# Attention and mixture-of-experts kernel: prologue and turn 0 written out by hand, and up's first high half moved from ScalarE to GpSimd

## The reference

```python
x = x + xattn(layernorm(x), ctx)          # q = xn Wq' + bq, k = ctx Wk' + bk, v = ctx Wv' + bv, softmax(q k' / sqrt(128)) v
h = layernorm(x)
probs = softmax(h router_w')
a_h = gelu(h actor_w1' + actor_b1)
k = argmax(clip(a_h actor_w2' + actor_b2, -30, 30)) + 1
scores = where(rank(probs) < k, probs, 0)
for e in range(8):
    out += scores[e] * ((silu(h gate_w[e]') * (h up_w[e]')) down_w[e]')
x = x + out
```

## Time and profile before

| what | value |
|---|---|
| median of 3 runs | 747.63 us (747.62 to 747.85) |
| the profiled execution | 748.23 us |
| its span | 746.3 us |
| PE busy | 736.3 us, 99% |
| DVE, ACT, POOL busy | 637.8, 558.8, 588.5 us |
| granted PE clock | 1.00 (2.4 GHz) in every stretch |

### The profile page before, as it was taken

The page is one execution under the profiler, slowest core; times in us unless marked ns, Lnnn a source line. Parts: engine busy times, 40 slices in busy tenths (PEclk is TensorE's granted clock), DMA queues, the critical chain, the costliest instruction groups (busy, mean ns, idle before and its releaser), DMA issues.

```text
span 746.3 us, 13836 instructions
## 1 busy us (share of the span) xinstructions
PE 736.3 (99%) x3680; PEld 363.5 (49%) x3680; DVE 637.8 (85%) x1407; ACT 558.8 (75%) x990; POOL 588.5 (79%) x616
## 2 busy tenths in 40 slices
PE   8999999999999999999999999999999999999998
PEld 4544454544545445454544545445454544444445
DVE  7899888897888889888898988889888897978777
ACT  5998787777877767777777777767777777877664
POOL 2686979789796887979698796887979688687763
PEclk9999999999999999999999999999999999999999
DMA  9200311314043142332424243152322323120110
GB/s 346 68 27 1 78 36 43 59 28 92 9 112 67 50 109 56 98 55 79 88 41 98 54 112 66 46 110 55 98 55 78 78 42 85 35 51 14 30 29 29
DMA packets 128511, 50.49 MB, mean 68 GB/s; under 512 B 106832, under 2 KB 117072, under 8 KB 128464
## 3 DMA queue, kind: packets, MB, share of 16 engines
q1 hardware_dynamic: 128032, 49.47, 27.8%
q10 hardware_dynamic: 432, 0.48, 0.2%
HBM read 28.92 MB, written 13.40 MB: 57 GB/s over the span
## 4 chain that ended last, share of the span: by engine, by line
PE 92%; ACT 2%; DVE 2%; issue 1%; DMA 1%; SPq 0%; POOL 0%; DVEq 0%; ACTq 0%; POOLq 0%
PE bank L690 28%; PE bank L692 28%; PE bank L691 28%; PE bank L586 2%; PE bank L557 2%; DMA raw_gate<-in_gate_t 1%; PE bank L651 1%; PE bank L670 1%; PE bank L594 1%; PE bank L593 1%; PE bank L595 1%; DVE bank L1663 0%; ACT up_hi L885 0%; DVE hid_lo L1669 0%; ACT down_hi L885 0%
## 5 line engine op out<-in xcount | busy, mean ns | idle before, releaser
L1288 POOL TENSOR_TENSOR weighted<-silu,score_bc 128x512 f32<-128x512 f32 x336 | 430.7, 1298 | 86.2 <-ACT silu L1037 81.7
L1663 DVE SCALAR_TENSOR_TENSOR bank<-bank,h_scale,weighted 128x512 f32<-128x512 f32 x336 | 253.5, 754 | 82.1 <-PE bank L692 66.8
L1031 ACT ACTIVATE hid_hi<-bank 128x512 f16<-128x512 f32 x336 | 200.8, 598 | 147.0 <-DVE bank L1663 144.9
L1037 ACT ACTIVATE silu<-bank,silu_scale 128x512 f32<-128x512 f32 x336 | 230.7, 687 | 23.3 <-PE bank L692 23.1
L1669 DVE TENSOR_TENSOR hid_lo<-bank,hid_hi 128x512 f16<-128x512 f32 x336 | 227.7, 678 | 0.0
L690 PE MATMUL bank<-xn_lo,gate_hi 128*128 128x512 f16 x336 | 127.6, 380 | 1.1 <-ACT silu L1037 1.0
L690 PE MATMUL bank<-xn_lo,up_hi 128*128 128x512 f16 x336 | 127.4, 379 | 1.2 <-DVE hid_lo L1669 0.9
L692 PE MATMUL bank<-xn_hi,up_hi 128*128 128x512 f16 x336 | 127.3, 379 | 0.0
L691 PE MATMUL bank<-xn_hi,up_lo 128*128 128x512 f16 x336 | 127.3, 379 | 0.0
L692 PE MATMUL bank<-xn_hi,gate_hi 128*128 128x512 f16 x336 | 127.3, 379 | 0.0
L691 PE MATMUL bank<-xn_hi,gate_lo 128*128 128x512 f16 x336 | 127.3, 379 | 0.0
(11 more groups left out here) (220 smaller groups left out, 809.6 us busy)
## 6 DMA issues: line engine op xcount, KB each, us to landing
x_in<-in_x SPq DMA_DIRECT2D x16, 256.0 KB, 2.8
y_kept<-y_sb SPq DMA_DIRECT2D x60, 64.0 KB, 2.6
y_tok<-y_kept SPq DMA_DIRECT2D x15, 256.0 KB, 2.8
out<-out_sb SPq DMA_DIRECT2D x15, 256.0 KB, 2.2
xt_in<-in_x_t SPq DMA_DIRECT2D x14, 256.0 KB, 2.9
row_bc<-row_kept SPq DMA_DIRECT2D x14, 256.0 KB, 4.0
ctx_in<-in_ctx_t SPq DMA_DIRECT2D x14, 240.0 KB, 2.9
v_kept<-raw_gate SPq DMA_DIRECT2D x10, 256.0 KB, 2.0
```

Source lines behind the costliest of these rows:

```text
L1031: af(hid_hi[j % HRING][:], up_bank[j % U_BANKS][:], ACT.Copy).then_inc(hid_hi_ready, 1)
L1037: af(silu[j % RING][:], gate_bank[(par + j) % G_BANKS][:], ACT.Silu, scale=silu_scale[:])\
L1288: g.tensor_tensor(weighted[j % RING][:], silu[j % RING][:], score_bc[par][:], ALU.mult)\
L1663: v.scalar_tensor_tensor(up_bank[j % U_BANKS][:], up_bank[j % U_BANKS][:], h_scale[:], weighted[j % RING][:], ALU.mult, ALU.mult).then_inc ...
```

## The change

Prologue and turn 0 are now one list of calls on each of PE, ACT, POOL and DVE; the loop over `j` begins with turn 1. On SP nothing changes. The tables of turn 0 and the helpers that made its exceptions are gone. No instruction is left out. One changes its engine: the high half of part 1 (up's first 7 tiles) is made by POOL. `value_bias(2)` goes from turn 0 into POOL's prologue, and block 1's values wait on `v_ready` (2) where they had a semaphore of their own.

```diff
 @block.tensor
+            values(0, 0, up_bank[2])
+            energies(0)
             keys(1, 1, up_bank[1])
-            energies(0)
-            values(0, 0, up_bank[2])
+            probs_transposes(0)
             values(1, 1, y_bank)
-            probs_transposes(0)
             attend(0)
...
-            gate(0, 0, 1)
-            gate(0, 0, 2)
-            score_transposes(0)
+            attend(1, y_bank)
             pe.wait_ge(kmin_ready, 1)
             keys(5, 1, x1)
+            gate(0, 0, 1)
+            score_transposes(0)
             score_broadcast(0)
-            attend(1, y_bank)
             up(0, 0, 0)
+            gate(0, 0, 2)
             up(0, 0, 1)
             gate(0, 0, 3)
+            gate(0, 0, 4)
             up(0, 0, 2)
...
 @block.scalar
             tanh(0)
-            keys(4, up_bank[0])
             exps(1)
-            weight_high(1)
+            weight_sums(7)
             router_exps(0)
+            keys(3, gate_bank[1])
+            turned_probs(1, up_bank[1])
             nc.scalar.preload_act_table(ACT.Silu)
             gated(0, 0, 0)
-            turned_probs(1, up_bank[1])
+            keys(4, up_bank[0])
             weight_high(2)
...
 @block.gpsimd
             rstd_2(0)
-            weight_high(0, 0, FIRST_TILES)
+            value_bias(2)
+            weight_high(0, 0, 2)
             x2_low(0, 0)
-            weight_high(0, FIRST_TILES, PART)
+            weight_high(0, 2, 7)
             route_probs(0)
+            weight_high(1, 0, 7)
             rank_over(0)
             pool.wait_ge(s16_ready, 1)
             rstd_1(2, 0)
             weigh(0, 0, 0)
+            weigh(0, 0, 1)
+            rstd_2(1)
+            weigh(0, 0, 2)
+            weigh(0, 0, 3)
+            weigh(0, 0, 4)
+            weigh(0, 0, 5)
+            add_row(2)
+            weigh(0, 0, 6)
...
+            weigh(0, 0, 12)
+            x2_low(1, 1)
+            route_probs(1)
...
 @block.vector
             weight_magnitude(0)
+            row_max(0)
             weight_magnitude(1)
-            row_max(0)
             row_below(0)
...
             router_sum(0)
+            values(1, y_bank)
             actor_count(0)
-            stats_1(2, 0, 2, BB)
             route_ahead(0)
             route_rank(0)
+            row_sum(1)
+            scores(0)
+            split_scores(0)
             aggregate_1_waits(2)
             aggregate_1(2)
-            scores(0)
-            split_scores(0)
-            values(1, y_bank)
             weight_low(1)
-            row_sum(1)
-            residual(1, 1, 0, BB, y_bank)
+            residual(1, 1, 0, 4, y_bank)
...
+            down_actor_scales()
+            weight_low(2)
+            hidden(0, 3)
+            low(0, 2)
+            weight_low(3)
+            hidden(0, 4)
+            low(0, 3)
+            hidden(0, 5)
+            low(0, 4)
+            weight_low(4)
...
```

More of the change, by code:

```diff
@@ L366, in turns @@
         def turns(eng, turn):
-            for t in range(LOOP_FIRST):
+            for t in range(1, LOOP_FIRST):
                 turn(t, t % 2)
@@ L1293, in turn @@
                 for j in range(TILES):
[L1295 removed]
+                    if j == 11 and is_block(t + 1):
                         route_probs(t + 1)
@@ new lines, in _ @@
+            stats_2_waits(1)
+            stats_2(1)
+            aggregate_2_waits(1)
+            aggregate_2(1)
+            hidden(0, 0)
+            weight_tops(1, 2, 3)
+            hidden(0, 1)
+            low(0, 0)
+            low(0, 1)
+            weight_top(1, 2, 4)
+            hidden(0, 2)
+            down_actor_scales()
[6 more added lines that the diff above has]
+            hidden(0, 5)
@@ new lines, in _ @@
+            low(0, 4)
+            weight_low(4)
+            low(0, 5)
+            hidden(0, 6)
+            actor_arg(1)
+            hidden(0, 7)
+            low(0, 6)
+            row_max(2)
+            actor_gelu(1)
+            weight_low(5)
+            row_base(2, 0)
+            hidden(0, 8)
+            hidden(0, 9)
+            low(0, 7)
+            router_less(1)
+            weight_low(6)
+            low(0, 8)
+            hidden(0, 10)
+            low(0, 9)
+            actor_logits(1)
@@ new lines, in _ @@
+            stats_1(3, 1)
+            actor_count(1)
+            hidden(0, 11)
+            low(0, 10)
+            router_sum(1)
+            weight_low(7)
+            hidden(0, 12)
+            low(0, 11)
+            low(0, 12)
+            aggregate_1_waits(3)
+            aggregate_1(3)
+            hidden(0, 13)
+            route_ahead(1)
+            hidden(0, 14)
+            row_sum(2)
+            weight_low(8)
+            route_rank(1)
+            hidden(0, 15)
+            low(0, 13)
@@ new lines, in _ @@
+            low(0, 14)
+            low(0, 15)
+            residual(2, 0, 0, 2)
+            scores(1)
+            hidden(0, 16)
+            residual(2, 0, 2, 4)
+            hidden(0, 17)
+            low(0, 16)
+            stats_2_waits(2)
+            stats_2(2)
+            hidden(0, 18)
+            low(0, 17)
+            aggregate_2_waits(2)
+            aggregate_2(2)
+            hidden(0, 19)
+            low(0, 18)
+            low(0, 19)
+            hidden(0, 20)
+            actor_low()
```

322 lines of the change are left out of this document (206 added, 116 removed).

## The result

| | kernel before | changed kernel |
|---|---|---|
| median | 747.63 us (747.40 to 747.96, 5 runs) | 752.31 us (751.66 to 753.16, 5 runs) |
| ratio | | 1.0063, 95% interval 1.0051 to 1.0074 |
| profiled execution | 748.23 us, span 746.3 | 752.31 us, span 750.5 |
| first up product | 33.00 us | 35.65 us |
| turn 1's first product, T0 | 79.71 us | 83.63 us |

The change makes the kernel 0.6% slower: 4.7 us where I forecast 0.3, and 2.7 us above the top of the range. Nearly all of it lies ahead of T0, as the prediction said: in the two profiled executions T0 moved by 3.92 us and the span by 4.2. The profiled executions lie 4.1 us apart and the medians 4.7, because that of the kernel before took 0.6 us more than its median and that of the changed kernel took just its median.

The account below looks back on a forecast made before the run. PE, busy for 99% of the span, was taken as the bound. First up product +1.0 us, one gate product more +0.65, fewer turn 0 stalls -1.4: +0.25 on 747.63 gives 747.9 us, range 746.3 to 749.6.

Parts of the forecast that it names:

- Only T0 can move: Whole kernel: PE has no gap from turn 1's first product (79.71 us), so only that start can move.
- `ahead` is held by POOL's high half: Prologue, DVE: ready at 28.6 us, `ahead` waits for POOL's `up_hi` until 30.4, some 2 us instead of 0.42.
- rival 2: Turn 0: low halves hit `add_row(2)` (part 3) and `weighted` 11 (part 6); 749.0 or 749.9 us; chance 0.20.
- "`value_bias(2)`" had no price: Turn 0: counted only as taken out of POOL's middle; no cost given for its new place in the prologue.
- `values(1)` fits into the wait for `probs_t`: nothing: Prologue, PE: `values(1)`, moved behind the transposes at 13.51 us, fits into the following wait and costs nothing.
- the row maximum, +0.25 us: Prologue, DVE: second maximum behind `row_max(0)`; the subtraction starts at 12.45 us, 0.25 us later.
- the score transposes, 32.65: Prologue, PE: score transposes start at 32.65 us instead of 30.36; 31.45 if `ahead` is not held.
- The reading of rows 8: Profile rows where DVE and POOL overlap: a held instruction begins its work only when the other engine's ends.
- turn 0, -1.4 us: Turn 0: PE's late starts sum to 1.0 us instead of 2.4, a gain of 1.4 us.
- the sign of an error: Turn 0: the forecast is wrong if PE's late starts sum to under 0.3 or over 2 us.
- Rival 1: Prologue: `ahead` isn't held and turn 0 flows; first up at 32.9 us, 746.2 us in all; chance 0.18.
- ACT's freed microsecond: Third rival, turn 0: reaching the silus it saves 0.45 us, 747.4; held not to; 0.62 together with the forecast.

Follow-up runs that it names:

- e4_before_high: The kernel before with only up's first high half moved from ACT to GpSimd, behind route_probs(0); 752.71 us (748.92 to 753.76).
- e16_high_filled: e4_before_high plus matmuls nobody reads, 3 ahead of gate(0, 0, 2) and 6 ahead of score_transposes(0); 748.79 us.
- e17_orders_alone: Changed kernel with up's first high half back on ACT, value_bias(2) back in turn 0, 4 unread matmuls in PE's wait at 12 to 14 us; 749.21 us.
- e18_row_back: e17_orders_alone with DVE's old order at the first row maximum, row_max(0) back behind weight_magnitude(1); 748.65 us.
- e7_filled: Changed kernel plus unread matmuls in PE's long waits: 4 ahead of probs_transposes(0), 3 and 3 around turn_x2(0), 3 ahead of score_transposes(0); 750.98 us.
- e14_tiles_back_filled: e7_filled with up's first high half back on ACT and value_bias(2) back behind weigh(0, 0, 10); 749.72 us.
- e1: Changed kernel with value_bias(2) back in turn 0, behind weigh(0, 0, 10); 751.12 us (750.20 to 752.63).
- e2: Changed kernel with up's first high half on POOL ahead of route_probs(0) instead of behind it; 751.49 us.
- e9: e7_filled with value_bias(2) back in turn 0, up's high half ahead of route_probs(0), and add_row(2) behind weigh(0, 0, 7); 758.00 us.
- e12_before_bias: The kernel before with value_bias(2) moved from turn 0 into GpSimd's prologue, behind rstd_2(0); 747.81 us.

## Why the prediction was wrong

**Held.** Only T0 can move, the rest follows it. `ahead` is held by POOL's high half, 1.88 us (forecast about 2). Part 3's low half against `add_row(2)`, rival 2's first half: POOL was first by 0.1 us, the low half took 2.38 us (forecast 2.5), and PE waited 0.77 (forecast 1.2). The other low halves of turn 0 came out of POOL's way, 1.12 to 1.14 us but for part 2's 1.70.

**Where the miss lies.** T0 was to be 79.9 and came at 83.63, 3.7 us later: 1.6 us of that are there at the score transposes, 2.1 come behind them. The two failures are what the sum left out; the rest are terms of it that were too small.

**Failed: "`value_bias(2)`" had no price.** I listed it only as taken out of turn 0's middle, and never asked what it meets where it goes. It meets `norm2(0)` and holds it by 0.95 us, on the chain to the scores; in the medians its return is worth 0.3 us with all waits filled, and 0.8 together with the filling that it makes needless. The Trainium skill says in "SBUF — State Buffer", § "SBUF: two separate sides", that a DVE instruction in a two-port mode is locked out by a GpSimd instruction just as one with two SBUF inputs. I had quoted that section, and used only its second case. The row at 20.04 shows a `tensor_scalar` on fp32 held so, 1287 ns for the held piece and 333 to 340 for the others; that it was in such a mode no row shows.

**Failed: "`values(1)` fits into the wait for `probs_t`: nothing".** It does fit, and it leaves PE 2.13 us without work in front. I priced waits by their length alone. The granted clock stood at 1.00 in every stretch, and I took it as given. It fell in every one of the changed kernel's executions, which is worth 1.3 us in the median; that wait is one of three places behind which it can come, as said above. The Trainium skill, "TensorE: Matmul & The Clock Gate", § "What's actually happening", says that the clock gate follows how busy PE has been; `e4_before_high` and `e16_high_filled` show it here, 752.71 and 748.79 us.

**Mis-sized: the row maximum, +0.25 us.** The medians of `e17_orders_alone` and `e18_row_back` show 0.56. I took the first `w_abs` at 9.35 from the profiled execution; it waited there 0.43 us for its DMA, and in `e17_orders_alone` it starts at 8.96. The wait for the energies, which the old order covers, was hidden by that.

**Mis-sized: the score transposes, 32.65.** They came at 34.26. With the waits filled, at full clock (`e7_filled`), it is 33.45: 0.38 us of the difference are there at the first transposes already (14.13 against 13.75), since that execution's first keys start at 7.80 us and those of the kernel before at 7.26. `norm2(0)` and the filling ahead of `turn_x2(0)` add about 0.95, and 0.5 come back, 0.3 of it since `up_hi` took 1.68 us and not 2.0: scaling from 640 columns overshoots. The other 0.81 go with the clock. The reading of rows 8 was a little off as well: an `up_lo` of 1.14 us that began at 47.65 would have taken 1.60 us from 47.19 and took 1.41, so a held instruction ends sooner behind its holder than I assumed.

**Mis-sized: turn 0, -1.4 us.** Late starts were to sum to 1.0 us; they sum to some 3.0 (47.98 - 44.95), over the 2 us that I had named as the sign of an error, and to the same at full clock in `e7_filled`. The first `weighted` was to come 0.8 us behind the first up and came 1.55 behind it (37.20), where before it came 0.2 ahead. The first up now comes 1.39 us behind the score transposes instead of 2.64, and `weighted` 2.94 instead of 2.42, since it stands behind `rstd_1(2)`, whose first instruction `ve` starts later behind them (DVE's `aggregate_1(2)` now follows the scores) and was itself held, 0.96 us. Part 3's low half adds the 0.77 us above. What makes the rest of the 2 us no run separates.

**The rivals.** Rival 1 fell with `ahead`. Rival 2 was the nearest, with half its mechanism and the wrong place for most of the price. That ACT's freed microsecond would help nobody fits the runs: with the copy back on ACT the time falls, by 1.0 us.

## What to carry to other kernels

When an instruction is moved between GpSimd and another place, look at what VectorE does at the new place, with every form that can be held, and by when its input arrives in the new order: the same place in a list was free in one prologue and held a DVE instruction of the scores' chain by 0.95 us in the other. A gap in TensorE's work is not priced by its length: where a reordering lets waits grow from about 1 to about 2 us, count the chance of some microseconds more for the clock (1.3 us here, 3.9 in `e4_before_high`), and look at the mean clock of every execution and not only the profiled one. Filling the waits with matmuls nobody reads tells the clock's share apart, less what the filling costs (0.5 us between `e14_tiles_back_filled` and `e17_orders_alone`).

## What the hardware did that I had not expected

- The clock fell in a kernel whose PE is busy for 98% of the span, in its prologue behind waits of 0.6 to 2.13 us, and in variants of it not in every execution: `e4_before_high` took 748.92 us at 1.000 and 753.76 at 0.995. In the profiles of the changed kernel, `e1`, `e2`, `e4` and `e9` the fall is of one size: the granted clock is 0.83 over 10 us (at 20, 30, 10, 30 and 50 us).
- A GpSimd instruction is held by DVE as well, even one of 4 columns: `ve` 0.96 us instead of 0.20 beside `up_lo`. And a DVE instruction of 2 columns is held by GpSimd: `w_mul` 0.85 us instead of 0.16 beside `value_bias(2)` in `e12_before_bias`.
- DVE's held instruction ends just behind GpSimd's: in the changed kernel `ahead` starts at 30.58 and ends at 32.46, 0.28 us behind the end of `up_hi`.
- The first keys start at 7.07 us in `e17_orders_alone` and at 7.80 in `e18_row_back`, which are the same up to there. PE's first 12 matmuls, of 512 columns, take 4.11 us in the one and 5.30 in the other, though the profile shows a granted clock of 1.00 for both.
